# One hybrid kernel on Trainium2: sums of x and a bias made once and kept in DRAM, together with a new table of slots

## The reference, cut to what matters

```python
x = x + mamba(_layernorm(x))      # layer a: has ff_ln_w and ff_ln_b in its last norm
x = x + experts(_layernorm(x))    # e1: 8 heads, one expert row of 8192 fetched per token and head
x = x + gated_scan(_layernorm(x)) # layer b
x = x + experts(_layernorm(x))    # e2: same weights as e1

def mamba(x):                     # cut
    xn = x * rsqrt(mean(x * x) + 1e-05) * norm_w
    u, res = split(xn @ in_proj_w.T, 2)
    u_c = silu(conv(u) + conv_b)
    dbl = u_c @ x_proj_w.T
    delta = softplus(dt_r @ dt_w.T + dt_b)
    # scan over 512 tokens, 256 channels, 16 states:
    h = exp(delta * A) * h + (delta * u) * B_t;  y_t = sum_n h * C_t
    out = (y + u_c * Dp) * silu(res) @ out_proj_w.T + x
    z = gelu(out @ ff_w1.T + ff_b1) @ ff_w2.T + ff_b2 + out
    return (z - mean(z)) * rsqrt(var(z) + 1e-05) * ff_ln_w + ff_ln_b
```

## Time and profile before

| | us |
|---|---|
| median of 3 runs | 2234.53 (2227.17 to 2236.09) |
| the profiled execution | 2228.89 |
| its span, first to last instruction | 2227.1 |
| iteration 0 (CORE of batch 0) | 79.4 |
| one iteration in the loop | about 119.5 |
| iteration 15 (CORE of batch 15) | 139.1 |
| tail | 318.9 |

### The profile page before, as it was taken

How to read it: one execution, slowest core, us unless ns; L and a number is a source line. 1 busy time by engine, 2 the same in 40 slices (tenths; PEclk the granted TensorE clock), 3 DMA queues, 4 the chain that set the end, 5 groups by cost and what they waited for, 6 DMA issues and landing times. The chain is left out here.

```text
span 2227.1 us, 25054 instructions
## 1 busy us (share of the span) xinstructions
PE 1687.7 (76%) x6098; PEld 948.0 (43%) x6188; DVE 1713.8 (77%) x4269; ACT 1508.2 (68%) x3248; POOL 1359.8 (61%) x1209
## 2 busy tenths in 40 slices
PE   4877777878897978888887888897979786644553
PEld 2333434344544545454444444444545453422432
DVE  3888888989897979898888889888989786422231
ACT  4656576769786868787787868686878664333442
POOL 0225454567776767776776767776777666545354
PEclk8899898989898989999999999899999887766776
DMA  2001111122322222322222232222232222222122
GB/s 53 0 10 48 38 48 39 48 71 76 86 76 76 76 77 76 90 76 75 75 77 79 67 88 72 84 76 82 74 88 71 82 64 67 82 63 81 48 80 76
DMA packets 79902, 151.06 MB, mean 68 GB/s; under 512 B 20584, under 2 KB 46592, under 8 KB 79680
## 3 DMA queue, kind: packets, MB, share of 16 engines
q0 software_dynamic: 49152, 134.28, 21.1%
q1 hardware_dynamic: 29344, 14.65, 2.4%
q10 hardware_dynamic: 1248, 0.34, 0.1%
HBM read 145.01 MB, written 4.19 MB: 67 GB/s over the span
## 5 line engine op out<-in xcount | busy, mean ns | idle before, releaser
L1498 POOL DMA_INDIRECT rows<-in_experts,index x1024 | 983.0, 960 | 456.8 <-issue 281.5
L1386 DVE TENSOR_TENSOR_SCAN hp<-dA,fed_ps 128x1024 f32<-128x1024 f32 x256 | 583.1, 2278 | 7.3 <-issue 5.7
L812 PE MATMUL ysum<-hp,ident 128*128 128x512 f32 x1024 | 498.1, 631 | 12.9 <-DVE hp L1396 12.9
L1513 POOL TENSOR_TENSOR hp<-hp,c_row 128x1024 f32<-128x1024 f32 x112 | 263.9, 2356 | 361.6 <-ACT c_row L1071 254.1
L1370 DVE TENSOR_TENSOR fed_ps<-du,b_ps 128x1024 f32<-128x1024 f32 x256 | 313.0, 1223 | 112.0 <-remote 51.5
L1056 ACT ACTIVATE dA<-delta,decay 128x511 f32<-128x511 f32 x512 | 334.5, 710 | 23.8 <-issue 21.8
L1035 ACT ACTIVATE rows<-rows,coef 128x128 f32<-128x128 f32 x1024 | 310.9, 390 | 7.6 <-DVE coef L1305 7.1
L812 PEld LDWEIGHTS ysum<-hp,ident 128*128 128x128 f32 x1024 | 211.3, 207 | 242.2 <-issue 209.1
L1298 DVE CUSTOM_DVE_ANT_0 rows<-rows,xn 128x128 f32<-128x128 f32 x1024 | 261.7, 318 | 33.3 <-DMA rows<-in_experts,index 22.3
L743 PE MATMUL bank<-rows,ident 128*128 128x256 f32 x1024 | 257.9, 410 | 21.9 <-ACT rows L1035 18.7
L962 ACT ACT_TABLE_LOAD x190 | 243.8, 1283 | 8.2 <-PEq L570 5.0
(11 more groups left out here) (186 smaller groups left out, 2350.8 us busy)
## 6 DMA issues: line engine op xcount, KB each, us to landing
rows<-in_experts,index POOLq DMA_INDIRECT x1024
x_in<-in_x SPq DMA_DIRECT2D x16, 256.0 KB
x_res<-in_x SPq DMA_DIRECT2D x16, 256.0 KB
y<-x SPq DMA_DIRECT2D x16, 256.0 KB
rows<-in_taps SPq DMA_DIRECT2D x1, 512.0 KB
rows<-in_wq_t SPq DMA_DIRECT2D x1, 512.0 KB, 5.5
rows<-in_in_proj_t ACTq DMA_DIRECT2D x1, 256.0 KB
rows<-in_key_t SPq DMA_DIRECT2D x1, 128.0 KB, 5.6
```

Of the source, the lines that this page charges most:

```text
L812: mm = nc.tensor.matmul(ysum[:, j, :], ident[:], hp[:, BUFFER[k], j, :], start=(k == order[0]), stop=(k == order[-1]))
L1386: nc.vector.tensor_tensor_scan(flat, dA[:, n % NDA, :, :].rearrange("p a b -> p (a b)"), fed_ps[:].rearrange("p a b -> p (a b)"), 0.0, ALU ...
L1498: pool.indirect_dma_start(e.rows[:, t, h, :], None, A["experts"], bass.IndirectOffsetOnAxis(ap=e.index[:, t, h:h + 1], axis=0)).then_inc(e ...
L1513: pool.tensor_tensor(state, state, c_row[:].unsqueeze(1).to_broadcast([P, NH, T]), ALU.mult).then_inc(pool_read, 1)
```

## The change

It has two parts.

1. In iteration 0, SP loads all 16 batches of x into the row buffer of e2 (L672 of the kernel after), POOL adds `ln_b` to each (L1542), and SP writes the sums to a new DRAM tensor `x_shifted`. One load stands at every fourth slot, one addition two slots after it, and the store of a batch before the load of the batch three further on. The last three stores stand in iteration 1, and the first load of `x_res` waits for all the stores. From then on `x_res` is loaded from `x_shifted`, POOL's addition in every batch is gone, and `dve_x1` waits for the load itself. POOL's first fetch of e2 also waits for the stores.
2. Nearly all numbers of `SLOTS` and `LAST_SLOTS` are new.

```diff
+SHIFT_SLOTS, SHIFT_LAG = TURN // NB, 3
...
-    "pe_ff1": (POST, (3,)),
-    "pe_ff2": (POST, (3,)),
+    "pe_ff1": (POST, (0,)),
+    "pe_ff2": (POST, (5,)),
...
+        def all_x(m):
+
+            tile, pair = divmod(m, NT)
+            return e2.rows[:, tile, 2 * pair:2 * pair + 2, :].rearrange("p h (a d) -> p (h a) d", d=P)
...
                 for slot in range(TURN):
+                    if isinstance(i, int) and i == 0 and slot % SHIFT_SLOTS == 0:
+                        m = slot // SHIFT_SLOTS
+                        if m >= SHIFT_LAG:
+                            sp.wait_ge(a_shift, m - SHIFT_LAG + 1)
+                            sp.dma_start(A["x_shifted"][m - SHIFT_LAG], all_x(m - SHIFT_LAG)).then_inc(shifted_out, 16)
+                        sp.dma_start(all_x(m), A["x"][m]).then_inc(all_in[m], 16)
                     for m, r, _ in due("sp_xres", i, q, slot):
                         if later(m):
                             sp.wait_ge(x1_done, at(m - 1, 1))
+                        else:
+                            for k in range(NB - SHIFT_LAG, NB):
+                                sp.wait_ge(a_shift, k + 1)
+                                sp.dma_start(A["x_shifted"][k], all_x(k)).then_inc(shifted_out, 16)
+                            sp.wait_ge(shifted_out, 16 * NB)
                         sp.dma_start(x_res[:].rearrange("p (a d) -> p a d", a=NT),
-                                     A["x"][m]).then_inc(xres_loaded, 16)
+                                     A["x_shifted"][m]).then_inc(xres_loaded, 16)
...
-                        dve.wait_ge(a_shift, at(m, 1))
+                        dve.wait_ge(xres_loaded, (m + 1) * 16)
...
+                if e is e2 and not later(n) and part == 0:
+                    pool.wait_ge(shifted_out, 16 * NB)
...
-                    for m, r, _ in due("pool_x1", i, q, slot):
-                        rows = x_res[:].rearrange("p (t d) -> p t d", t=NT)
-                        pool.wait_ge(xres_loaded, (m + 1) * 16)
-                        pool.tensor_tensor(rows, rows, ln_b[:].unsqueeze(1).to_broadcast([P, NT, P]),
+                    if isinstance(i, int) and i == 0 and slot % SHIFT_SLOTS == 2:
+                        m = slot // SHIFT_SLOTS
+                        if m == 0:
+                            pool.wait_ge(weights_in, 16 * LOADS)
+                        pool.wait_ge(all_in[m], 16)
+                        pool.tensor_tensor(all_x(m), all_x(m), ln_b[:].unsqueeze(1).to_broadcast([P, NT, P]),
                                            ALU.add).then_inc(a_shift, 1)
```

More of the change, by code:

```diff
@@ L106 @@
+    "act_dbl": (PRE, (30,)),
+    "act_soft": (PRE, (40, 47)),
+    "act_split": (PRE, (36, 37)),
+    "act_exp": (PRE, (48,)),
+    "act_ln": (PRE, (52,)),
+    "act_out": (POST, (3,)),
+    "act_gelu": (POST, (3,)),
+    "act_rstd_a": (POST, (4,)),
+    "act_rstd_e1": (POST, (29,)),
+    "act_norm_e1": (POST, (36,)),
+    "act_turn_e1": (POST, (29,)),
+    "act_flip_e1": (POST, (42, 51)),
+    "act_gelu_e1": (POST, (66, 84)),
+    "act_scale_e1": (POST, (79, 81, 93, 93)),
     "act_out_e1": (POST, (91, 98)),
-    "act_rstd_b": (POST, (104,)),
@@ L151 @@
     "pe_out": (POST, (0,)),
-    "pe_ff1": (POST, (2,)),
-    "pe_ff2": (POST, (4,)),
-    "pe_ln_a": (POST, (8,)),
+    "pe_ff1": (POST, (1,)),
+    "pe_ff2": (POST, (7,)),
+    "pe_ln_a": (POST, (14,)),
     "pe_turn_e1": (POST, (19,)),
-    "pe_sim_e1": (POST, (25, 32, 41, 41)),
-    "pe_flip_e1": (POST, (37, 41)),
-    "pe_code_e1": (POST, (37, 54)),
-    "pe_sum_e1": (POST, (80, 90)),
-    "pe_turn_b": (POST, (118,)),
-    "pe_xp": (POST, (119,)),
-    "pe_gate": (POST, (123,)),
+    "pe_sim_e1": (POST, (34, 38, 44, 46)),
@@ L181 @@
-    "act_rstd_b": (POST, (104,)),
-    "act_norm_b": (POST, (116,)),
-    "act_turn_b": (POST, (120,)),
-    "act_xp": (POST, (127,)),
+    "act_rstd_e1": (POST, (29,)),
+    "act_norm_e1": (POST, (53,)),
+    "act_turn_e1": (POST, (19,)),
+    "act_flip_e1": (POST, (42, 51)),
+    "act_gelu_e1": (POST, (62, 89)),
+    "act_scale_e1": (POST, (82, 82, 91, 91)),
+    "act_out_e1": (POST, (91, 98)),
+    "act_rstd_b": (POST, (110,)),
+    "act_norm_b": (POST, (119,)),
+    "act_turn_b": (POST, (122,)),
@@ L185 @@
+    "act_xp": (POST, (123,)),
     "act_gate": (POST, (127,)),
     "act_tanh": (POST, (128,)),
[L187 to L197 removed]
@@ L203 @@
+    "dve_x1": (POST, (14,)),
+    "dve_stats_e1": (POST, (16,)),
+    "dve_shift_e1": (POST, (36,)),
+    "dve_top_e1": (POST, (39, 40, 44, 45)),
+    "dve_index_e1": (POST, (42, 51)),
+    "dve_dot_e1": (POST, (54, 58, 76, 76)),
+    "dve_weigh_e1": (POST, (71, 85)),
+    "dve_stats_b": (POST, (106,)),
     "dve_shift_b": (POST, (108,)),
     "dve_scan_b": (POST, (126,)),
-    "dve_x3": (POST, (144,)),
-    "dve_stats_e2": (POST, (152,)),
-    "dve_shift_e2": (POST, (178,)),
-    "dve_top_e2": (POST, (165, 169, 185, 185)),
@@ L502, in build @@
         a_shift = sem("a_shift")
+        all_in = [sem(f"all_in{m}") for m in range(NB)]
+        shifted_out = sem("shifted_out")
         x1_done = sem("x1_done")
```

197 lines of the change are left out of this document (90 added, 107 removed).

## The result

| | before | after |
|---|---|---|
| median of the runs, us | 2235.31 (4 runs, 2227.17 to 2247.38) | 2329.05 (4 runs, 2324.05 to 2340.06) |
| ratio after to before | | 1.040, 95% interval 1.035 to 1.045 |
| up to the gate of iteration 0, us | 131.5 | 130.9 |
| iterations 1 to 3 together | 321.9 | 306.3 |
| iterations 4 to 14 together | 1315.8 | 1452.2 |

I had forecast 2178 us. The stretches are distances between DVE's gates (now L1501), as before. Iterations 1 to 3, which have no fetches of e2 yet, are 15.6 us faster together, iteration 15 is 12.9 us faster, and iterations 4 to 14, which have everything, lose 136.4 us, 12.4 us each on average.

What follows compares the result with a forecast made beforehand. DVE was taken to pace the loop, busy 104.7 of 119.2 us an iteration with about 14.5 idle. The terms -35 - 24 + 12 - 6 - 3 = -56 us gave 2178 us for the median, range 2135 to 2222.

Steps and rivals of the forecast that it cites:

- the first term: POOL's addition out of each batch: taken as 0, bounds 0 and a gain of 1 us a batch, 15 in all.
- rival A: Loop head: the hold moves with `pe_ff2`, so the feed of state 3 waits 2 us or more; 2205 to 2210; chance 0.18.
- The term of -35: Loop head: `pe_ff2` behind slot 4 removes the wait of state 2's feed; -35 us, bounds 57 and 16.
- a gain of 24: L1449 ahead of the scan of state 1 no longer collides with POOL's multiplication; 24 us, bounds 0 and 26.
- the other side of that account: Collisions of DVE's dots behind POOL, about 1.7 us a batch, only move: taken as 0, bounds -20 and +20.
- +12 for new short waits: Rest of the loop: DVE arrives earlier than some PE or ACT work; 1 us in each of twelve full iterations.
- Iteration 0, iteration 15, tail: Iteration 0 still about 79 us; iteration 15 -6, its similarities ahead of a sum; tail -3, bounds -18 and +15.
- Table loads: Two more a batch on ACT, 2.6 us a batch on an engine idle 25: taken as 0 besides 0.6 at the head.
- C: Slower: ACT late at slots 44 to 47 with the second expert's gelu, stopping DVE's weigh; +22, 2256 us; chance 0.10.
- theory S: From the experiments: PE's second sum of the second expert (slot 57), ahead of ACT's last scaling (slot 60), holds the spreads.
- B: No change: new short waits in the experts' chains may eat the head's gain; 2234, within 11; chance 0.12.

Runs made afterwards that it cites:

- e6: Kernel before with only POOL's addition per batch removed (`ln_b` left out of the result), no sums in DRAM: 2322.0 us, 1.038 to before.
- e1: Part 1 alone: the code of after with `SLOTS` and `LAST_SLOTS` of before: 2325.3 us, 1.044 to before.
- e9: Kernel before, with POOL pausing after every four fetches until they have landed, batches 0 to 10: 2305.1 us, 1.054 to before.
- e2: As a run, not the expert: kernel before with the new slots only, addition in every batch, `sp_xres` at slot 4: 2209.7 us, 0.994 to before.
- e13: Kernel after run again unchanged, on a chip where before takes 2050.7 us: 2005.2 us, 0.976 to before.
- e3: Kernel after with ACT's last two scalings of the second expert at slots 50 and 55 in place of 55 and 60: 2329.4 us, 1.042 to before.
- e17: Kernel before run again unchanged, on a fifth chip: 2052.2 us, 1.000 to before.
- e14: Kernel after with each fetch bringing 512 bytes for a partition in place of 1024, result not the reference's: 2000.6 us.
- e18: Kernel after with half the bytes in every fetch, run on a fifth chip: 2002.9 us, 0.977 to before.
- e12: Kernel after plus a POOL wait for the gate at slot 0, with three small DVE steps moved from under POOL's multiplications: 2164.1 us, 0.989 to before.

## Why the prediction was wrong, step by step

- **The bounds of the first term are where it failed.** For the addition taken out of each batch I wrote "I take 0. The bounds are 0 and a gain of 1 us a batch, 15 in all." No loss at all was let in. On the chips with the hold it is a loss of 81 us in e6, where nothing else is touched, and of 94 in e1. The reason that I gave, that POOL still waits 2.67 us for `c_row` and so is early, was true and did not bear on it. What counted was not when POOL ends but whether its fetches are interrupted.
- **What holds PE.** "I can't say what holds PE, but it holds whatever follows `pe_ff2`." It was POOL's row of fetches, and it holds signals of PE and DVE alike (e9: `pe_ff2` in place, pauses on POOL, wait gone; on the chips without the hold the same feed waits 0.4 us with `pe_ff2` in place). Moving `pe_ff2` did what I forecast for the feed of state 2, and rival A's wait at the feed of state 3 did not come in iterations 5 to 14 (0.0 us). But the hold did not "belong to the moment" by chance: it follows the row, and the row went from 8 to 16.
- **The term of -35.** In e2, the slots without part 1, unrecorded waits of feeds fall from 51.5 us over the run to 5.5. So the term was of the right kind. The saving was used up by the holds under POOL and by new waits, of which the feed of state 10 has 23.4 us in ten iterations. A misreading stands under the term: the line at 1776.68 in the earlier trace rows is the feed of state 1 and not "the same feed", which waits 2.13 us at 1783.36. The fifteen waits come to 55.1 us and not 57.1.
- **L1449.** Median 0.160 us: right. As a gain of 24 it was mis-sized, since the other side of that account was put at 0 with bounds of 20: the weighs lose 4.0 us an iteration in after, the dots 1.0 more than before and L1418 1.3, some 63 us in ten iterations. I named the dots and neither the weighs nor L1418; the second weigh of e1 went from slot 21 to 24, which is a slot of POOL's, and that of e2 from 49 to 45.
- **+12 for new short waits.** On the chips without the hold this can be read alone: 2.6 us an iteration less busy time of DVE, 2.8 more idle. The charge should have been nearly three times mine.
- **Iteration 0, iteration 15, tail.** 79.3 us against "about 79"; -12.9 us where I took -6 (-21.4 on the chips without the hold); +3.9 where I took -3, within my bounds.
- **Table loads.** Two more a batch cost nothing that I found: in e13 the load ends at 1211.60 and the next activation starts at 1211.62. The 1.38 us of drain in the Trainium skill, "ScalarE: Activation LUTs", section "What ACT_TABLE_LOAD costs", is not seen at this place either.
- **Rivals.** A did not happen. C, slower, named the right sign and the wrong mechanism: ACT's gelu is not what DVE waits for in the loop, the feed of state 13 waits 0.0 us there, and e3 excludes theory S. B's argument, that new short waits eat the gain of the head, holds for the loop of the two chips without the hold.
- **What I could have known.** That a row of fetches ends just ahead of the late signals is in the trace of before, at 1183.76. That some chips don't have the hold is not: no trace that I had shows it. On those the kernel after stands at 0.976, and my forecast of 2178 against 2234 was 0.975. That is luck: 47 of my 56 us were to come from the head of all fifteen iterations, less new waits, and there iterations 5 to 14 are 2 us longer together. The gain came from iterations 1 to 3 (-15.6), 15 (-21.4) and the tail (-2.4), and e17 and e13 are single traces on two chips.

The holds of DVE under POOL are what the Trainium skill, "SBUF — State Buffer", section "SBUF: two separate sides", states: DVE and GpSimd share a pair of ports, and of a DVE instruction with two inputs in SBUF and a GpSimd instruction that reads SBUF the one that starts first has the pair for its whole length, while the other stands. The rows at 1018 and 1027 us agree that DVE stands for the whole of POOL's 2.36 us; not that the first to start wins, since by the recorded starts DVE's rows are ahead, by 0.04 and 0.48 us. The same section says that PE never waits on anyone, by which it means these ports; the rows show PE issuing in time and its signals late, which is another matter.

## What to carry to other kernels

Work or a wait that seems to be idle weight on one engine may be what separates two rows of another kind: before taking it out, look at what becomes one uninterrupted row and who waits for a signal while that row runs. When several engines wake at one moment, look for what ended just before on *any* engine, POOL's indirect DMAs first. And compare on more than one chip: this change is 4.0% slower on one and 2.4% faster on another.

## What the runs showed of the hardware that I had not expected

- In four of six comparisons, while POOL issues indirect DMAs back to back (0.95 us each, 0.30 between), PE's semaphore increments come late and arrive in a burst 1.5 to 3 us after the row ends; in the row shown DVE goes on 10.5 us after PE started, where 0.42 is enough in e13. DVE's own increments are held too (2.45 us at 1003.81). The engines act on the late increments, so this is no error of the records. Rows of 4 show none of it, rows of 8 some, and in rows of 16 13 increments per ten rows get through from 10 to 22 us after the start.
- A pause of 3.7 us (2.42 of waiting and 1.26 of an addition) lets them through, a memset does not. What lies between was not tried.
- Whether it is the issuing or the landing bytes, and what differs between the chips, stays open: e14 and e18, made for the first, ran on chips where nothing is held. Records of PE's matmuls don't tell the kinds apart: the traces of e9 to e12 have all 6188 and show the hold.
- The records of increments do. For increments that come from DMAs, the fourteen traces with the hold (before, after, e1 to e12) have 5775 to 9683, the six without it (e13 to e18) 17,680 to 18,223, with as many fetches in all of them; the traces with rows of 4 have the most of the fourteen. Of DVE's increments after has 1440 and e13 1720. So where signals are late, records of signals are lost.
- That leaves a rival which nothing here excludes: that the recording of the increments is what holds them. Every time in this document comes with a span and a clock from such a recording, and no run shows what these kernels take without it. The runs show that the row of fetches without a pause brings the loss about in such a recorded execution; whether it would in one that isn't recorded is open.
